# First feed-forward weight loaded at the end of the cross stage, into the place of its FiLM weights

## The reference, cut to what matters

```python
x = _layernorm(x + attn(x))                                  # linear attention
# cross part, x_text = x
attn_mean = top-32 softmax over the context, mean of 4 heads
c_t = (attn_mean @ (x_vision @ Wv)) * text_mask
y = layernorm(x) * (1 + gate * scale_in(c_t)) + gate * shift_in(c_t)
y = s4d(y)                                                   # a long convolution, by FFT
y = y * (1 + gate * scale_out(c_t)) + gate * shift_out(c_t)
xt = x_text + y
h = gelu(layernorm(xt) @ W1 + b1) @ W2 + b2                  # W1: 512 x 2048, W2: 2048 x 512
x = _layernorm(x + layernorm(xt + h))
x = _layernorm(x + bitlinear(silu(conv1d(bitlinear(x, w1))), w2))
```

## Time and profile before

| | us |
|---|---|
| median of 3 runs | 4627.98 |
| lowest and highest | 4618.25, 4632.38 |
| profiled execution, its own time | 4627.62 |
| its span in the profile | 4625.7 |
| attention | 0 to 743 |
| prepare | 743 to 958 |
| cross | 958 to 3124 |
| feed_forward | 3125.64 to 4625.7 |

### The profile page before, as it was taken

One profiled execution on the slowest core, in us unless ns is written; L12 is line 12 of the kernel. 1 busy time (PEld: TensorE's weight loads), 2 busy tenths in 40 slices (PEclk: granted clock), 3 DMA queues, 4 the chain that ended last, 5 costly groups with the idle time before them and its releaser, 6 DMA issues. The chain is left out here.

```text
span 4625.7 us, 72165 instructions
## 1 busy us (share of the span) xinstructions
PE 4098.6 (89%) x28037; PEld 3012.6 (65%) x28066; DVE 3605.4 (78%) x4993; ACT 2086.2 (45%) x3944; POOL 1714.8 (37%) x2132
## 2 busy tenths in 40 slices
PE   8999995669999999999999999985888998989984
PEld 6777772337777677777777777774566666666652
DVE  5666666859999999999999999672577766766767
ACT  3334332135555555555555555412354544544543
POOL 1111113712332255655556565502342333333320
PEclk9999997758999899999999999987899999999997
DMA  2111114230111111121112111235311112111101
GB/s 85 53 49 47 51 47 160 83 119 28 37 37 37 60 40 42 46 65 39 34 49 67 37 39 31 89 75 198 124 46 52 50 51 61 51 40 61 46 23 38
DMA packets 216422, 276.08 MB, mean 60 GB/s; under 512 B 96899, under 2 KB 144707, under 8 KB 212560
## 3 DMA queue, kind: packets, MB, share of 16 engines
q1 hardware_dynamic: 198674, 216.92, 15.7%
q0 software_dynamic: 17408, 54.56, 3.3%
HBM read 186.44 MB, written 84.98 MB: 59 GB/s over the span
## 5 line engine op out<-in xcount | busy, mean ns | idle before, releaser
L1953 PE MATMUL f_p_g<-f_hT,f_w 128*128 128x128 f32 x4096 | 536.6, 294 | 68.2 <-ACT f_gT L2053 53.7
L1953 PEld LDWEIGHTS f_p_g<-f_hT,f_w 128*128 128x128 f32 x4096 | 525.2, 210 | 88.7 <-ACT f_gT L2053 56.6
L1194 PEld LDWEIGHTS c_p_a<-c_diag,c_s 128*128 128x128 f32 x4096 | 515.7, 207 | 55.0 <-issue 43.4
L1194 PE MATMUL c_p_a<-c_diag,c_s 128*128 128x128 f32 x4096 | 528.9, 292 | 17.3 <-ACT c_s L1394 9.2
L1961 PE MATMUL f_p_o<-f_w,f_gT 128*128 128x512 f32 x1024 | 481.8, 592 | 0.0
L1373 ACT ACTIVATE c_s<-c_p_s 128x512 f32<-128x512 f32 x512 | 280.9, 590 | 417.7 <-PE c_p_s L1185 298.8
L1246 PEld LDWEIGHTS c_p_m<-c_aT,c_vals 128*128 128x128 f32 x3072 | 350.1, 192 | 40.5 <-issue 40.5
L1246 PE MATMUL c_p_m<-c_aT,c_vals 128*128 128x128 f32 x3072 | 364.2, 277 | 2.1 <-ACT c_aT L1405 2.1
L1265 PE MATMUL c_p_m<-c_wf,c_uT 128*128 128x512 f32 x768 | 357.0, 600 | 2.5 <-ACT c_uT L1410 1.6
L1184 PE MATMUL c_p_s<-c_kt,c_qT 32*128 32x512 f32 x1024 | 344.6, 692 | 14.4 <-ACT c_s L1373 14.1
L1541 DVE TENSOR_TENSOR c_z<-c_s 128x1024 f32<-128x1024 f32 x256 | 330.7, 1292 | 0.0
(11 more groups left out here) (379 smaller groups left out, 8866.2 us busy)
## 6 DMA issues: line engine op xcount, KB each, us to landing
mod_out<-c_fo POOLq DMA_DIRECT2D x32, 512.0 KB, 3.3
f_mr<-mod_out SPq DMA_DIRECT2D x32, 512.0 KB, 4.6
p_ct<-in_ctxT SPq DMA_DIRECT2D x16, 768.0 KB, 5.0
c_vals<-in_ctx SPq DMA_DIRECT2D x4, 3072.0 KB, 12.2
c_kb<-kspec SPq DMA_DIRECT2D x22, 512.0 KB, 3.7
a_xt<-in_xT SPq DMA_DIRECT2D x32, 256.0 KB, 3.1
a_xr<-in_x SPq DMA_DIRECT2D x32, 256.0 KB, 2.6
x<-a_out POOLq DMA_DIRECT2D x32, 256.0 KB, 2.5
```

What stands on the lines that cost most here:

```text
L1194: last = mm(p_a[:, n, :], s[:, j % RING, n * P:(n + 1) * P], diag[:, j % 2, :], start=(h == 0 and n % 4 == 0), stop=(h == NH2 - 1 and n % ...
L1953: last = mm(p_g[:, f % 8, :], w1[:, k, f * P:(f + 1) * P], hT[:, k * P:(k + 1) * P], start=(k == 0 and f % 4 == 0), stop=(k == KD - 1 and ...
```

## The change

W1's buffer and a semaphore `w1_in` are made in `decoder`, in a context that spans both of the last stages. `cross` uses the buffer under other names: its first three quarters are `wf`, its last quarter is `fm`. In the loop over the last five pairs SP issues, behind pair i's store and the spectrum load that follows it, a load of a quarter of W1 (i = 0 to 3, 1 MB each), the first behind a wait for the last FiLM product. `feed_forward` no longer loads W1. W2 gets a semaphore `w2_in`; `ff_in` has seven DMAs left. `up` waits for `w1_in` at the first group of every tile, `down` for `w2_in`. The outer context ends with its own semaphore clear and barrier.

```diff
-def cross(nc, x1, xn, keysT, ...
+def cross(nc, shared, W1, x1, xn, keysT, ...
-        wf = m.sb("wf", [P, KV3, 4 * D])
+        w1, w1_in = shared
+        flat = w1[:].rearrange("p k n -> p (k n)")
+        wf = flat[:, 0:KV3 * 4 * D].rearrange("p (k n) -> p k n", k=KV3)
-        fm = m.sb("fm", [P, RX, 2, P])
+        fm = flat[:, KV3 * 4 * D:].rearrange("p (n r c) -> p n r c", n=RX, r=2)
...
                 if i + 2 < REST:
                     load_spectrum(i + 2)
+                if i == 0:
+                    sp.wait_ge(fo_done, TILES)
+                if i < KD:
+                    sp.dma_start(w1[:, i, :], W1[i * P:(i + 1) * P, :]).then_inc(w1_in, 16)
...
-        w1 = m.sb("w1", [P, KD, F])
+        w1, w1_in = shared
...
             sp.dma_start(b1c[:], b1T).then_inc(ff_in, 16)
-            sp.dma_start(w1[:], W1.rearrange("(k p) n -> p k n", p=P)).then_inc(ff_in, 16)
             load_tile(1)
             load_mod(1)
-            sp.dma_start(w2[:], W2.rearrange("(k p) n -> p k n", p=P)).then_inc(ff_in, 16)
+            sp.dma_start(w2[:], W2.rearrange("(k p) n -> p k n", p=P)).then_inc(w2_in, 16)
...
             def up(t, f):
                 if f == 0:
+                    pe.wait_ge(w1_in, 16 * KD)
                     pe.wait_ge(hT_copied, t + 1)
...
             def down(t, f):
                 if f == 0:
+                    pe.wait_ge(w2_in, 16)
                     at_least(pe, var[1], t)
...
-            pe.wait_ge(ff_in, 16 * 9)
+            pe.wait_ge(ff_in, 16 * 7)
... (the same on ACT, VectorE and GpSimd)
+    with ExitStack() as ctx:
+        m = Alloc(nc, ctx, "w_")
+        w1 = m.sb("w1", [P, KD, F])
+        w1_in = m.sem("w1_in")
+        cross(nc, (w1, w1_in), a["W1"], ...)
+        feed_forward(nc, (w1, w1_in), ...)
```

More of the change, by code:

```diff
@@ L891, in idft8_tail, with cross @@
     return tt(v[:, 1, 7], t[:, 1, 6], q[:, 1, 1], ALU.subtract)
-def cross(nc, x1, xn, keysT, values, film_w, film_b, mask_row, text_mask, Wq, eye, xm, mod_out, conv_k, D_skip, dft, idft,
+def cross(nc, shared, W1, x1, xn, keysT, values, film_w, film_b, mask_row, text_mask, Wq, eye, xm, mod_out, conv_k, D_skip, dft, idft,
           dft4, idft4, kspec, ys):
@@ L1090, in _ @@
             load_values(0)
-            sp.dma_start(wf[:], film_w.rearrange("(k p) n -> p k n", p=P)).then_inc(film_in, 16)
+            sp.dma_start(wf, film_w.rearrange("(k p) n -> p k n", p=P)).then_inc(film_in, 16)
             load_xn(0)
@@ L1094, in _ @@
             sp.dma_start(dsk[:], D_skip.rearrange("(a n) -> a n", a=1)).then_inc(dft_in, 16)
-            sp.dma_start(fm[:], dft).then_inc(dft_in, 16)
+            sp.dma_start(fm, dft).then_inc(dft_in, 16)
             sp.dma_start(gm[:], idft).then_inc(dft_in, 16)
@@ L1726, with feed_forward @@
 WB = 2 * P
-def feed_forward(nc, x1, ys, mod_out, W1, b1T, W2, b2, g_ffn, b_ffn, g_out, b_out, eye, x2, q1T, inv_rows,
+def feed_forward(nc, shared, x1, ys, mod_out, b1T, W2, b2, g_ffn, b_ffn, g_out, b_out, eye, x2, q1T, inv_rows,
                  w1T, w2T, conv_w, conv_b, out):
@@ L1803, in feed_forward @@
         p_y = m.ps("p_y", [P, D])
-        (ff_in, consts, h_ready, hT_done, hT_copied, g_done, g_copied, o_done, mod_done, step, pstep, qb_ready, qT_done,
+        (ff_in, w2_in, consts, h_ready, hT_done, hT_copied, g_done, g_copied, o_done, mod_done, step, pstep, qb_ready, qT_done,
          qT_copied, x2_ready, r3_ready, ln_head, out_norm, inv_done) = [m.sem(n) for n in (
-             "ff_in consts h_ready hT_done hT_copied g_done g_copied o_done mod_done step pstep qb_ready qT_done "
+             "ff_in w2_in consts h_ready hT_done hT_copied g_done g_copied o_done mod_done step pstep qb_ready qT_done "
              "qT_copied x2_ready r3_ready ln_head out_norm inv_done").split()]
@@ L2075, in _ @@
             root(0, 0)
-            act.wait_ge(ff_in, 16 * 9)
+            act.wait_ge(ff_in, 16 * 7)
             copy_h(0)
@@ L2119, in _ @@
             v.memset(ones[:], 1.0).then_inc(consts, 1)
-            dve.wait_ge(ff_in, 16 * 9)
+            dve.wait_ge(ff_in, 16 * 7)
             v.tensor_copy(identb[:], ident[:]).then_inc(consts, 1)
@@ L2335, in _ @@
             tt = pool.tensor_tensor
-            pool.wait_ge(ff_in, 16 * 9)
+            pool.wait_ge(ff_in, 16 * 7)
             st = Steps(pool, pstep, 0)
@@ L2413, in decoder @@
             a["log_dt"], a["A_re"], a["A_im"], a["C_re"], a["C_im"], a["angles"], conv_k)
[L2414 to L2417, removed]
+    with ExitStack() as ctx:
+        m = Alloc(nc, ctx, "w_")
+        w1 = m.sb("w1", [P, KD, F])
+        w1_in = m.sem("w1_in")
+        cross(nc, (w1, w1_in), a["W1"], x1, xn, keysT, a["ctx"], film_w, film_b, mask_row, a["mask1"], a["Wq"], a["eye"], xm, mod_out,
+              conv_k, a["D_skip"], a["dft"], a["idft"], a["dft4"], a["idft4"], kspec, ys)
+        feed_forward(nc, (w1, w1_in), x1, ys, mod_out, a["b1T"], a["W2"], a["b2"], a["g_ffn"], a["b_ffn"], a["g_out"],
+                     a["b_out"], a["eye"], x2, q1T, inv_rows, a["w1T"], a["w2T"], a["conv_w"], a["conv_b"], a["out"])
 def transform_matrices():
```

## The result

The changed kernel takes 4604.12 us (median of 6 runs, 4601.9 to 4607.39) against 4629.1 us for the kernel before (6 runs, 4618.25 to 4632.38): a ratio of 0.995, 95% interval 0.994 to 0.9961, 25.0 us. I had predicted 4605.5, in 4597 to 4618, against 4627.98.

The account below looks back on a forecast made before the run. The feed-forward start was taken to hang on W2, last of nine DMAs on ff_in, queued behind W1. From 4627.62 us, -23.30 for the shared wait and +1.1 for the outer context gave 4605.4; predicted 4605.5, range 4597 to 4618.

Parts of the forecast that it names:

- The shared wait: Feed-forward start: engines wait on ff_in for b1c's landing at 3137.44 instead of W2's at 3160.74; -23.3 us.
- W1 and W2 in time: First up and down: W1 in SBUF by 3109, W2 by 3150.6, both before they are wanted; 0 us.
- Four loads in the convolutions: Last convolution pairs: four 1 MB W1 loads behind spectrum loads stay hidden; 0 us taken, at most 17 us.
- Added waits: TensorE's 64 waits for w1_in and w2_in in the tiles stay hidden; 0 us taken, at most 3.3 us.
- TensorE's clock: First up keeps its loss from a granted clock of 0.84; if that went, up to 2.7 us more gain.
- The outer context: End of the kernel: one more semaphore clear and barrier, between 0.3 and 1.1 us; +1.1 us taken.
- All that follows moves as one piece: After down(0, 0) everything shifts together; uncertainty about 7 us either way, from DMA links in slots 1 to 3.
- A: Slots 1 to 3: opening gain repaid as two quick DMA links become slow, +12.8 us, 4618 us; chance 0.12.
- B: Last convolution pairs: SP stands at the W1 loads, last store late, adds 9 to 11 us, about 4615.5; chance 0.08.
- C: Feed-forward tiles: TensorE runs dry at every added wait, 67 us added, 4672 us; chance 0.05.
- D: Feed-forward start doesn't move, b1c or a broadcast landing with the bulk behind it; 4618 to 4629 us; chance 0.02.

Follow-up runs that it names:

- e4_ahead: The changed kernel with W1's quarters issued ahead of the spectrum loads, two behind each of the first two pairs' stores: 4602.36 us, ratio 0.995.
- e3_once: The changed kernel with the waits for w1_in and w2_in only at the first tile, 62 waits fewer: 4600.76 us, ratio 0.9943.
- e1_split: The kernel before with only the semaphores split (w1_in, w2_in, ff_in with seven DMAs), W1 still loaded inside feed_forward: 4603.95 us, ratio 0.9948.

## Why the prediction was right, and what it missed

*The shared wait, -23.3: right.* The start of `up`, counted from the stage's first issue, went from 47.21 to 24.03 us, -23.18; `b1c` landed at 3137.39 against 3137.44.

*W1 and W2 in time, 0: right.* Neither is in the chain. A quarter of W1 took 5.3 to 7.8 us from issue to landing, not 2.5 to 4.2. The tightest place covers even that: the second quarter, issued at 3072.49, had landed by 3080.3, 1.9 us ahead of SP's next store at 3082.23. The 10 us of free queue that I had claimed behind each were 9.7 there.

*Four loads in the convolutions, 0: right*, with e4_ahead as the counter-test: 2.5 us in its profile, where they stand ahead of the spectra.

*Added waits, 0: right*, by e3_once. In the changed kernel a wait of 51 ns at line 1967 stands in the first tile too, at 3164.2, ahead of its product at 3166.23.

*TensorE's clock, left in: right.* The first `up` still took 16.81 us, at a clock of 0.86, against 17.16 at 0.84.

*The outer context, +1.1: too much.* In the changed kernel the first of the two releases of SP at line 82 is at 4605.1, the second at 4605.5: 0.4 us, near the lower bound. The stage's own clear and barrier take 1.1 us here too (4604.0 to 4605.1); what differs is the number of semaphores to clear, one against a stage's many.

*All that follows moves as one piece: wrong by 3.3 us, within the range.* At tile 1 the changed kernel is 23.63 us ahead, at tile 8 23.93, at tile 9 22.32, and from tile 10 on 20.6 to 20.7. The DMA links of the earlier trace rows are not the cause (the last is 9.61 us in the changed kernel against 10.55, the largest 10.72 against 11.28): it is the clock of tiles 8 and 9, 0.91 and 0.96 against 0.96 and 1.00. The prediction's margin for what comes after the start was drawn from the DMA links, and took no account of this one. The sum in the profiles: -0.09 stage boundary, -23.18 to `up`, -0.35 in the first `up` and its neighbourhood, -0.3 to tile 8, +3.3 clock, +0.4 outer context = -20.2. The medians differ by 25.0. The 4.8 us between the two are not explained by any run: they may come from executions in which the earlier stages and the clock fell otherwise, for the start of the stage alone varies by 10.6 us between the profiles. So the gain of 22.2 was forecast 2.0 us above what the profiles show and 2.8 below the medians, and that the median came within 1.4 us of 4605.5 is in part luck.

*The rivals.* A, B, C and D did not come: no repayment in slots 1 to 3, SP stands at most 1.15 us at a W1 load, no dry starts, and the start moved. (Tiles 1 to 3 take 102.1 us together before and 102.5 after.)

*What the prediction missed* is in its own numbers. It has W1 landing 16.8 us after its issue at 3130.42, at 3147.2, and `up` at 3149.55. So W1 loaded at its old place would have been 2.3 us ahead of its reader, and the larger part of the change, the early load with its shared buffer, was worth nothing beside the semaphores. e1_split showed it, to the few us that these medians can tell. A case "half of the change does it all" belonged among the rivals.

## What to carry to other kernels

Before moving a transfer, look at what waits for it: a semaphore that counts small constants and large weights together holds every engine for the largest, and splitting it by first reader cost two waits and gave 23 us here. Then compare each transfer's landing with its first reader's new start; only one that is late there is worth loading earlier (here 3.7 us at its reader's start, and only after the waits for the constants had been placed by their readers too). Put such a load behind the loads that the running stage still waits for, not ahead: here that was the spectra's order.

## What the runs showed of the hardware

A gain at one place is not carried to the end unchanged: with equal work and nearly equal gaps (3.3 and 3.2 us) TensorE's mean granted clock over tile 9 was 1.00 in the kernel before and 0.96 in the changed one, 44.04 against 45.65 us, and the tile from which it stays at 0.96 and 0.91 was tile 7, 8 or 10 (counted from 0), depending on the profile. The Trainium skill, "TensorE: Matmul & The Clock Gate", section "Part 1: The HAM clock gate (the "warmup" mystery)", says that the monitor behind the clock runs freely and isn't restarted by the kernel, so that the same kernel can have a different number of slow products from run to run. The tiles above fit it, but no kernel here was profiled twice, so they don't show it.

A transfer of 1 MB behind other traffic of the same queue took 5.3 to 7.8 us from issue to landing, while by the 416 GB/s that the queue moved in bulk the same bytes are 2.5 us. A context of its own around two stages costs 0.4 us at the end.
